# Attention over 32 batch items: LayerNorm pieces, value and key units and the text keys' scores in other places of a step

## The chip, the cores and the metric

The kernel runs on one core of a Trainium2 chip. Its five engines are named as in the profile: PE (TensorE, matmuls; PEld are its weight loads), DVE (VectorE), ACT (ScalarE), POOL (GpSimd) and SP (SyncE, which here only issues DMAs). Each works through a list of its own in order and waits on semaphores. The metric is the device time of one execution in microseconds (us); lower is better.

## What is computed

A state-space kernel gives 128 image rows per batch item, 77 text rows are put behind them, and these 205 rows go through causal attention and a linear layer with a Fourier adapter:

```python
h = _L0_tok_ref(L0_tok_log_dt, L0_tok_Lambda, x, 1024)      # (32, 128, 1024)
h = jnp.concatenate([h, txt], axis=1)                       # (32, 205, 1024)
h = h + _L0_attn_ref(_layernorm(h, axis=-1), wq, wk, wv, wo)
h = h + _L0_ffn_ref(_layernorm(h, axis=-1), W_base, b_base, ...)
```

The attention has 32 query heads of 32 channels and 8 key/value heads, so 4 query heads share a key head. The softmax is over the keys j <= i.

## The kernel before

The program has three stages: `ssm` (the state-space part), `attention`, and `tail` (output projection and linear layer). The change is in the first two, nearly all of it in `attention`.

**Steps and slots.** `attention` is software-pipelined over the batch. Step b (from -4 to 32) works on several items at once: attention proper of item b ("att"), row maxima of item b+1 ("max"), projections of item b+2 ("qkv"), transposes of item b+3 ("turn"), LayerNorm of item b+4 ("ln"), the load of item b+5. A step has eight slots g, one for each key head. Every float32 operand is split into a high and a low float16 part, and a product is three matmuls.

**PE in slot g.** The list of a slot: `scores(g, 0)` and `scores(g, 1)` (transposed scores, image keys, L981; called S0 and S1 here), `score_rows(g, 0)` and `(g, 1)` (scores for the row maxima, L1024 and L1028: M0, M1), the first half of a projection unit (FRONT, 12 matmuls), `scores(g, 2)` (text keys, L984: S2), `score_rows(g, 2)` (M2, which begins with L1028), the second half (BACK), `weigh(g-1)` (weights times values, 36 small matmuls: W), and then the slot's further units. A unit is 24 matmuls of 205 columns. Each slot has a query unit; `EXTRA` adds a value or key unit to four slots, and two "m" units (two small transposes each) stand in slots 0 and 4.

**The two banks of the transposed scores.** S0, S1 and S2 write PSUM banks `psT` in turn, so each waits until ACT's exponential has read the bank two before it:

```python
wait(pe, exp_done, 24 * b + 3 * g + k - 1)
ps = psT[(g + k) % 2]
```

So S2 of slot g waits for the exponential of part 0 of g, and S1 of slot g+1 waits for the exponential of part 2 of g.

**ACT in slot g** takes the exponentials of the three parts (L783), copies the three parts to their high float16 half (L790) once POOL has masked them, then copies the slot's units out of PSUM (L798). `high_part` (L732, L734: centre and scale half a row tile) stands behind slots 4 to 7. ACT's queue also issues `load`, `store` and `values` (the two copies L742).

**POOL in slot g** masks the three parts (`affine_select`, L699), each when its exponential is there, and then takes the low half of parts 1 and 2 (L704). After slot 3 it runs `scale_rows`: twelve small operations for 1/sqrt(variance) and one for the mean (L1135 to L1138, L673).

**DVE in slot g** reduces M0 (L879), M1, takes the low half of the unit left over from the slot before (L893), reduces M2, takes the low half of part 0 (L936), does its LayerNorm work (`layer_norm` in slots 1 to 3; `low_part`, L862, in slots 6, 7 and 0), normalizes W's result of slot g-1, and splits the slot's units but the last. In slot 7 it splits the last one too, before the M0 of the next step:

```python
if m < len(rows[g]) - 1 or g == NKV - 1:
    split_unit(*late)
```

**SP** restacks keys and queries, issues the DMA transposes of the LayerNorm output (`turn`) and of the values, and shifts the maxima rows. At step 30 it issues fifteen loads for the tail (`ahead`).

## Time and profile before

| what | value |
|---|---|
| three runs, us | 2894.34, 2895.55, 2897.94 (median 2895.55) |
| the profiled execution, its time, us | 2894.3 |
| its span, us | 2891.9 |
| PE busy, share of the span | 92% |
| DVE, ACT, POOL busy, share of the span | 67%, 43%, 40% |
| mean granted PE clock | 0.975 of full |

Some 2.4 us lie around the span. Busy shares are means over three stages that differ: in the attention loop all four engines have much to do, in the tail PE works nearly alone.

### The profile page before, as it was taken

What the parts mean: (1) busy time and instruction counts of PE and PEld (TensorE: products, weight loads), DVE (VectorE), ACT (ScalarE), POOL (GpSimd) and SP (SyncE); (2) the same over time, 40 slices, a digit from 0 to 9 for tenths busy, and PEclk for the clock granted to TensorE, in tenths of its full rate; (3) what the DMA queues carried; (4) which work ended last, traced back from release to release, by engine and by line L of the source; (5) the groups of instructions that cost most, each with busy time, mean ns of one, the idle gap of its engine ahead of it and who ended that gap; (6) DMA issues with size and microseconds to landing.
All of it is one profiled execution on the core that took longest, in us unless ns stands there. A gap on an engine that the chain in (4) does not pass through costs nothing. (4 is left out here: it accounts for less than half of the span.)

```text
span 2891.9 us, 70053 instructions
## 1 busy us (share of the span) xinstructions
PE 2655.3 (92%) x27456; PEld 1919.6 (66%) x27456; DVE 1941.2 (67%) x5569; ACT 1230.0 (43%) x2570; POOL 1144.9 (40%) x1810
## 2 busy tenths in 40 slices
PE   1948999999999999999999976999999999999999
PEld 1838888888888888888888952444444444444444
DVE  8966888888888888888888674644444444444443
ACT  4343676766767676766667572201000010101010
POOL 2751565656656565666656570101010101010100
PEclk9979999999999999999999976999999999999999
DMA  7756556465555555565555454454545455545553
GB/s 242 194 122 100 98 92 105 85 109 93 96 94 96 103 93 104 84 107 92 101 92 86 73 124 170 113 139 116 133 122 136 119 134 121 133 123 131 125 129 77
DMA packets 509031, 332.99 MB, mean 115 GB/s; under 512 B 421145, under 2 KB 464409, under 8 KB 508225
## 3 DMA queue, kind: packets, MB, share of 16 engines
q1 hardware_dynamic: 486192, 264.68, 46.3%
q10 hardware_dynamic: 22512, 63.84, 7.1%
q8 instruction: 219, 3.59, 0.6%
q14 instruction: 108, 0.88, 0.1%
HBM read 116.49 MB, written 80.61 MB: 68 GB/s over the span
## 5 line engine op out<-in xcount | busy, mean ns | idle before, releaser
L1044 PE MATMUL psJ<-xth,qh 128*128 128x205 f16 x2048 | 517.3, 253 | 51.6 <-DMA xtl<-xfl 47.6
L704 POOL TENSOR_TENSOR pl<-arena,ph 128x410 f16<-128x410 f32 (+1 forms) x512 | 501.0, 998 | 94.7 <-ACT ph L790 94.7
L1046 PE MATMUL psJ<-xth,ql 128*128 128x205 f16 x2048 | 516.3, 252 | 0.0
L1045 PE MATMUL psJ<-xtl,qh 128*128 128x205 f16 x2048 | 515.8, 252 | 0.0
L699 POOL TENSOR_SCALAR_AFFINE_SELECT arena<-arena 128x256 f32<-128x256 f32 (+1 forms) x768 | 331.7, 438 | 438.3 <-ACT arena L783 419.3
L1261 POOL TENSOR_TENSOR arena<-stage,arena 128x1024 f32<-128x1024 f32 x52 | 122.1, 2349 | 936.2 <-DVE stage L1304 936.2
L1275 ACT CAST xh<-arena 128x1024 f16<-128x1024 f32 x52 | 54.3, 1045 | 995.1 <-DVE arena L1313 995.1
L783 ACT ACTIVATE arena<-psT,escale 128x410 f32<-128x410 f32 (+1 forms) x768 | 399.6, 565 | 95.5 <-PE psT L984 57.5
L790 ACT CAST ph<-arena 128x410 f16<-128x410 f32 (+1 forms) x768 | 334.8, 500 | 14.9 <-POOL arena L699 14.7
L1304 DVE SCALAR_TENSOR_TENSOR stage<-ps5O,osc,h_in 128x512 f32<-128x512 f32 x104 | 77.9, 750 | 388.4 <-PE ps5O L1401 388.4
L885 DVE TENSOR_REDUCE mx<-psS 77x2 f32<-77x410 f32 x512 | 296.5, 579 | 60.7 <-PE psS L1031 57.0
L1399 PE MATMUL ps5F<-wfh,xth 128*128 128x512 f16 x832 | 315.4, 379 | 3.4 <-DMA xtl<-xl 2.3
L1400 PE MATMUL ps5O<-wol,ath 128*128 128x512 f16 x832 | 316.1, 380 | 0.0
L1399 PE MATMUL ps5O<-woh,ath 128*128 128x512 f16 x832 | 316.1, 380 | 0.0
L1401 PE MATMUL ps5O<-woh,atl 128*128 128x512 f16 x832 | 316.0, 380 | 0.0
L1400 PE MATMUL ps5F<-wfl,xth 128*128 128x512 f16 x832 | 315.3, 379 | 0.0
L1401 PE MATMUL ps5F<-wfh,xtl 128*128 128x512 f16 x832 | 315.3, 379 | 0.0
L879 DVE CUSTOM_DVE_ANT_0 seen<-psS,mask 128x128 bf16<-128x128 f32 x1024 | 235.4, 286 | 82.7 <-PE psS L1024 82.0
L1010 PE MATMUL psO<-vh,ph 128*128 128x33 f16 (+1 forms) x3072 | 261.0, 178 | 5.0 <-issue 4.6
L1010 PE MATMUL psO<-vl,ph 128*128 128x33 f16 (+1 forms) x3072 | 260.0, 178 | 0.0
L1010 PE MATMUL psO<-vh,pl 128*128 128x33 f16 (+1 forms) x3072 | 260.0, 178 | 0.0
L1046 PE MATMUL psJ<-xth,kl 128*128 128x205 f16 x1024 | 257.8, 252 | 0.0
(231 smaller groups left out, 6106.2 us busy)
## 6 DMA issues: line engine op xcount, KB each, us to landing
a_in<-acat SPq DMA_DIRECT2D x52, 512.0 KB, 3.8
h_in<-hcat SPq DMA_DIRECT2D x52, 512.0 KB, 4.6
qst<-qsh SPq DMA_DIRECT2D x128, 205.0 KB, 4.7
out<-stage SPq DMA_DIRECT2D x51, 512.0 KB, 3.1
hcat<-ob SPq DMA_DIRECT2D x64, 256.0 KB, 4.4
xin<-hcat ACTq DMA_DIRECT2D x32, 512.0 KB
acat<-arena ACTq DMA_DIRECT2D x64, 256.0 KB
qst<-qsl SPq DMA_DIRECT2D x64, 205.0 KB, 5.7
```

What stands on the lines that cost most here:

```text
L699: pool.affine_select(out=v, in_=v, compare_op=ALU.is_ge, fill=0.0, base=0, pattern=[[0, v.shape[1]], [1, w]], channel_multiplier=-1).then_ ...
L704: pool.tensor_tensor(view(pl, g % 2, k), view(p32, g % 2, k), view(ph, g % 2, k), ALU.subtract).then_inc(lo_pool, 1)
L783: act.activation(view(p32, g % 2, k), ps_view(psT[(g + k) % 2], k), ACT.Exp, scale=(escale[:, 0:1] if k < 2 else escale[0:TXT, 0:1])).then ...
L790: act.copy(view(ph, g % 2, k), view(p32, g % 2, k)).then_inc(hi_done, 1)
L885: dve.tensor_reduce(dst, v, AX.X, ALU.max).then_inc(s_read, 1)
L1010: m = pe.matmul(o[:, t, r, :], p, v[0:T[j], j, g, :], start=n == 0, stop=n == len(list_) - 1)
L1044: pe.matmul(ps[:, 0:S], wh[:, k, c], xth[:, par, k, 0:S], start=k == 0, stop=False)
L1045: pe.matmul(ps[:, 0:S], wh[:, k, c], xtl[:, par, k, 0:S], start=False, stop=False)
L1046: m = pe.matmul(ps[:, 0:S], wl[:, k, c], xth[:, par, k, 0:S], start=False, stop=k == KC - 1)
L1399: pe.matmul(ps[h][:], th[:, k, :], wh[:, k, c], start=k == 0, stop=False)
L1400: pe.matmul(ps[h][:], th[:, k, :], wl[:, k, c], start=False, stop=False)
L1401: m = pe.matmul(ps[h][:], tl[:, k, :], wh[:, k, c], start=False, stop=k == KC - 1)
```

## The change

Four edits in `attention`, and one at its border with `ssm`.

1. `EXTRA` moves the value and key units from slots 0 to 3 to slots 1 to 4. `HIGH`, `LOW` and `LINK` set the LayerNorm pieces: ACT's `high_part` behind slots 1, 2 and 3 (two pieces there), DVE's `low_part` in slots 2, 3 and 4 (two pieces there), the statistics in slots 1 to 3. They now work on item b+3 in the step in which it is transposed, so `rs` and `nmean` have two buffers. POOL's `scale_rows` moves from behind slot 3 to behind slot 4.
2. On PE, S2 moves behind M2 and BACK.
3. On ACT the exponential of part 2 moves behind the high copies of parts 0 and 1. On POOL the low half of part 1 moves ahead of the mask of part 2.
4. `load` and `store` are issued by SP and not by ACT, `values` is split over slots 1 and 2, and SP's list is reordered; the loads for the tail are spread over the steps from 1 on.
5. Before the loop the first item's LayerNorm is done by DVE alone, its pieces come ahead of half of the weights' low parts, and item 0 is loaded alone. In `ssm` the weight peaks are taken two chunks earlier, and their way through memory starts a chunk earlier.

```diff
             for dst, src, arrived in ahead:
                 sp.dma_start(dst, src).then_inc(arrived, 16)
             for ch in range(NCH):
-                if ch == NCH - 1:
-
+
+                if ch == NCH - 2:
                     sp.wait_ge(peaks_ok, 1)
                     sp.dma_start(acat[0, 0:2 * P].rearrange("(p t) -> p t", t=2), peaks[:]).then_inc(peaks_out, 16)
+                if ch == NCH - 1:
                     sp.wait_ge(peaks_out, 16)
                     sp.dma_start(all_peaks, acat[0:1, 0:2 * P].broadcast_to([P, 2 * P])).then_inc(peaks_in, 16)
 
...
-        EXTRA = {0: ("v", 0), 1: ("v", 1), 2: ("k", 0), 3: ("k", 1)}
+        EXTRA = {1: ("v", 0), 2: ("v", 1), 3: ("k", 0), 4: ("k", 1)}
+
+
+        HIGH, LOW, LINK = {1: (0,), 2: (1,), 3: (2, 3)}, {2: (0,), 3: (1,), 4: (2, 3)}, {1: 0, 2: 1, 3: 2}
...
+                if has["last"]:
+                    store(b - 1, 1)
                 if has["qkv"]:
 
...
+                if has["turn"]:
+
+                    wait(sp, pj_filled, base)
+                    turn(0, nxt, b + 3)
+                if has["qkv"]:
+
+                    wait(sp, pj_lo, base + at(rows, "k", 0) + 1)
+                    wait(sp, st_filled, 24 * b + 12)
+                    restack(K_PARTS, kst[par][:, 0:4], slice(0, 1), k_in[0])
+                    wait(sp, pj_lo, base + at(rows, "q", 3) + 1)
+                    restack(Q_PARTS, qst[par][:, 0], HALVES[0], q_in[0])
+                if has["turn"]:
+                    turn(1, nxt, b + 3)
                 if has["max"]:
 
                     wait(sp, pj_lo, base + at(rows, "m", 0) + 1)
                     shift_rows(0, nxt)
+                if has["att"]:
+                    store(b, 0)
+                if has["load"]:
+                    sp.wait_ge(x_lo, 4 * (b + 4))
+                    load(b + 5, 1 - par)
+                if 1 <= b < len(ahead):
+                    dst, src, arrived = ahead[b]
+                    sp.dma_start(dst, src).then_inc(arrived, 16)
+                if b == B - 3:
+
+                    for q in v_in:
+                        sp.wait_ge(q, 32 * B)
+                    dst, src, arrived = ahead[0]
+                    sp.dma_start(dst, src).then_inc(arrived, 16)
+
...
+            load(0, 0)
+            sp.wait_ge(x_in[0], 32)
+            load(1, 1)
...
+            def causal(b, g, k):
+                pool.wait_ge(exp_done, 24 * b + 3 * g + k + 1)
+                v = view(p32, g % 2, k)
+                v = v[:, :, 0:P] if k < 2 else v
+                w = v.shape[2]
+                pool.affine_select(out=v, in_=v, compare_op=ALU.is_ge, fill=0.0, base=0,
+                                   pattern=[[0, v.shape[1]], [1, w]], channel_multiplier=-1).then_inc(masked, 1)
+
+            def low_weights(b, g, k):
+                pool.wait_ge(hi_done, 24 * b + 3 * g + k + 1)
+                pool.tensor_tensor(view(pl, g % 2, k), view(p32, g % 2, k), view(ph, g % 2, k),
+                                   ALU.subtract).then_inc(lo_pool, 1)
 
...
-                    for k in range(3):
-                        pool.wait_ge(exp_done, 24 * b + 3 * g + k + 1)
-                        v = view(p32, g % 2, k)
-                        v = v[:, :, 0:P] if k < 2 else v
-                        w = v.shape[2]
-                        pool.affine_select(out=v, in_=v, compare_op=ALU.is_ge, fill=0.0, base=0,
-                                           pattern=[[0, v.shape[1]], [1, w]],
-                                           channel_multiplier=-1).then_inc(masked, 1)
-                    for k in (1, 2):
-                        pool.wait_ge(hi_done, 24 * b + 3 * g + k + 1)
-                        pool.tensor_tensor(view(pl, g % 2, k), view(p32, g % 2, k), view(ph, g % 2, k),
-                                           ALU.subtract).then_inc(lo_pool, 1)
-                    if g == 3 and has["ln"]:
+                    causal(b, g, 0)
+                    causal(b, g, 1)
+                    low_weights(b, g, 1)
+                    causal(b, g, 2)
+                    low_weights(b, g, 2)
+                    if g == 4 and has["ln"]:
                         scale_rows(b)
 
...
+            def exponential(b, g, k):
+                act.wait_ge(st_filled, 24 * b + 3 * g + k + 1)
+
+                if k:
+                    wait(act, lo_pool, 16 * b + 2 * (g - 2) + k)
+                else:
+                    wait(act, lo_done, 8 * b + g - 1)
+                act.activation(view(p32, g % 2, k), ps_view(psT[(g + k) % 2], k), ACT.Exp,
+                               scale=(escale[:, 0:1] if k < 2 else escale[0:TXT, 0:1])).then_inc(exp_done, 1)
+
+            def high_weights(b, g, k):
+                act.wait_ge(masked, 24 * b + 3 * g + k + 1)
+                act.copy(view(ph, g % 2, k), view(p32, g % 2, k)).then_inc(hi_done, 1)
+
...
                 if b == -3:
+                    for n in range(4):
+                        high_part(0, n)
...
-                    if g == 3 and has["load"]:
-                        act.wait_ge(x_lo, 4 * (b + 4))
-                        load(b + 5, 1 - par)
-                    if g == 2 and has["last"]:
-                        store(b - 1, 1)
-                    if g == 2 and has["max"]:
-                        values(b + 1)
-                    if g == 6 and has["att"]:
-                        store(b, 0)
                     if has["att"]:
-                        for k in range(3):
-                            act.wait_ge(st_filled, 24 * b + 3 * g + k + 1)
-
-                            if k:
-                                wait(act, lo_pool, 16 * b + 2 * (g - 2) + k)
-                            else:
-                                wait(act, lo_done, 8 * b + g - 1)
-                            act.activation(view(p32, g % 2, k), ps_view(psT[(g + k) % 2], k), ACT.Exp,
-                                           scale=(escale[:, 0:1] if k < 2 else escale[0:TXT, 0:1])
-                                           ).then_inc(exp_done, 1)
-
+                        exponential(b, g, 0)
+                        exponential(b, g, 1)
                         wait(act, av_done, 8 * b + g - 1)
-                        for k in range(3):
-                            act.wait_ge(masked, 24 * b + 3 * g + k + 1)
-                            act.copy(view(ph, g % 2, k), view(p32, g % 2, k)).then_inc(hi_done, 1)
+                        high_weights(b, g, 0)
+                        high_weights(b, g, 1)
+                        exponential(b, g, 2)
+                        high_weights(b, g, 2)
+                    if g in (1, 2) and has["max"]:
+                        values(b + 1, g - 1)
...
-                    if g >= 4 and has["ln"]:
-                        high_part(b, par, g - 4)
+                    if has["turn"] and b > -3:
+                        for piece in HIGH.get(g, ()):
+                            high_part(b + 3, piece)
...
-                    if has["turn"] and g == 0:
-                        low_part(b + 3, 3)
-                    if has["ln"]:
-                        if g in (1, 2, 3):
-                            layer_norm(b, par, g - 1)
-                        if b == -4 and g == 3:
-                            weights_low(0)
-                        for piece in {6: (0,), 7: (1, 2)}.get(g, ()):
-                            low_part(b + 4, piece)
-                        if b == -3 and g == 0:
-                            weights_low(1)
+                    if b == -3 and g == 0:
+                        for part, ks in (((0, 1), (4, 5)), ((2, 3), (6, 7))):
+                            for piece in part:
+                                low_part(0, piece)
+                            weights_low(0, ks)
+                        weights_low(1, range(KC))
+                    if has["turn"] and b > -3:
+                        for piece in LOW.get(g, ()):
+                            low_part(b + 3, piece)
+                    if has["ln"] and g in LINK:
+                        layer_norm(b, par, LINK[g])
+                    if b == -4 and g == NKV - 1:
+                        weights_low(0, range(4))
...
                     project(0, FRONT)
+                    maxes(groups[:1], (2,))
+                    project(0, BACK)
                     if has["att"]:
                         scores(b, par, g, 2)
-                    maxes(groups[:1], (2,))
-                    project(0, BACK)
                     maxes(groups[1:], (0, 1))
                     if has["att"] and g:
                         weigh(b, par, g - 1)
```

Where the rows stand now. The names are those of the program: `arena` holds the exponentials in float32, `ph` and `pl` their high and low float16 parts, `psJ` a unit, `qsh`, `ksh` and `mh` its high part. ACT, from the end of slot 3 into slot 5, before:

```order
L798 CAST ksh<-psJ 128x205
L783 ACTIVATE arena<-psT,escale 128x410 x2
L783 ACTIVATE arena<-psT,escale 77x308
L790 CAST ph<-arena 128x410 x2
L790 CAST ph<-arena 77x308
L798 CAST qsh<-psJ 128x205
L796 ACTIVATE mh<-psJ 16x205
L732 ACTIVATE xin<-xin,nmean 128x512
L734 ACTIVATE xfh<-xin,rs 128x512
L783 ACTIVATE arena<-psT,escale 128x410 x2
```

The same place after, from the end of slot 3 through slot 4:

```order
L826 CAST ksh<-psJ 128x205
L761 ACTIVATE xin<-xin,nmean 77x512
L763 ACTIVATE xfh<-xin,rs 77x512
L761 ACTIVATE xin<-xin,nmean 77x512
L763 ACTIVATE xfh<-xin,rs 77x512
L785 ACTIVATE arena<-psT,escale 128x410 x2
L790 CAST ph<-arena 128x410 x2
L785 ACTIVATE arena<-psT,escale 77x308
L790 CAST ph<-arena 77x308
L826 CAST qsh<-psJ 128x205
L826 CAST ksh<-psJ 128x205
L824 ACTIVATE mh<-psJ 16x205
```

Two pieces of row work now stand ahead of slot 4's exponentials, and the third exponential stands between the second and the third high copy.

POOL around `scale_rows` (`rs` holds its intermediate values), before, the end of slot 3 and the start of slot 4:

```order
L704 TENSOR_TENSOR pl<-arena,ph 128x410
L704 TENSOR_TENSOR pl<-arena,ph 77x308
L1135 TENSOR_TENSOR rs<-rs 128x2
...
L673 TENSOR_SCALAR nmean<-mv 128x2
L699 AFFINE_SELECT arena<-arena 128x2x128 x2
L699 AFFINE_SELECT arena<-arena 77x308
L704 TENSOR_TENSOR pl<-arena,ph 128x410
```

After, the end of slot 4 and the start of slot 5:

```order
L720 TENSOR_TENSOR pl<-arena,ph 77x308
L1172 TENSOR_TENSOR rs<-rs 128x2
...
L706 TENSOR_SCALAR nmean<-mv 128x2
L715 AFFINE_SELECT arena<-arena 128x2x128 x2
L720 TENSOR_TENSOR pl<-arena,ph 128x410
L715 AFFINE_SELECT arena<-arena 77x308
L720 TENSOR_TENSOR pl<-arena,ph 77x308
```

The thirteen small operations stand one slot later, and the low half of part 1 is ahead of the text keys' mask.

## Rows read from the trace of the kernel before

**Rows 1.** The page's first line.
```profile
span 2891.9 us, 70053 instructions
```

**Rows 2.** Windows: steps 0 to 27, and step 31. Columns: busy time (x instructions), clock.
```profile
286.80:1588.90 1302.10, 1227.55 (x19119) 1148.37 (x19117) 1072.87 (x3666) 896.80 (x2019) 799.06 (x1483) 1.00 0.56 96
...
1712.10:1740.00 27.90, 18.95 (x314) 10.97 (x314) 21.79 (x37) 22.85 (x49) 23.73 (x39) 0.50 0.09 32
```

**Rows 3.** Timeline, PE, steps 13 and 14. Columns: start, length, line, what.
```profile
898.26 0.51 PE L981 MATMUL psT<-qst,kst 98*128 98x410 f16 x2
...
904.62 0.51 PE L981 MATMUL psT<-qst,kst 98*128 98x410 f16 x2
...
918.61 0.51 PE L981 MATMUL psT<-qst,kst 98*128 98x410 f16 x2
...
923.03 0.51 PE L981 MATMUL psT<-qst,kst 98*128 98x410 f16 x2
...
925.46 0.33 PE L984 MATMUL psT<-qst,kst 98*77 98x308 f16 x1 [0.19 <-ACT arena L783]
...
927.84 0.51 PE L981 MATMUL psT<-qst,kst 98*128 98x410 f16 x2
...
937.07 0.51 PE L981 MATMUL psT<-qst,kst 98*128 98x410 f16 x2
...
938.96 0.30 PE L984 MATMUL psT<-qst,kst 98*77 98x308 f16 x1
...
940.34 0.23 PE L1028 MATMUL psS<-mask,ident_bf 77*77 77x154 bf16 x1 [1.09 <-DVE mx L879]
```

**Rows 4.** Timeline, ACT, the end of slot 3 to slot 6, step 13.
```profile
918.81 0.33 ACT L798 CAST ksh<-psJ 128x205 f16<-128x205 f32 x1 [2.39 <-PE psJ L1046]
...
921.76 1.32 ACT L790 CAST ph<-arena 128x410 f16<-128x410 f32 x3 [0.41 <-POOL arena L699]
...
923.46 0.70 ACT L732 ACTIVATE xin<-xin,nmean 128x512 f32<-128x512 f32 x1
...
924.83 1.51 ACT L783 ACTIVATE arena<-psT,escale 128x410 f32<-128x410 f32 x3
926.24 1.30 ACT L790 CAST ph<-arena 128x410 f16<-128x410 f32 x3
927.45 0.32 ACT L798 CAST qsh<-psJ 128x205 f16<-128x205 f32 x1
```

**Rows 5.** Timeline, POOL, slots 3 to 7 of step 13.
```profile
917.77 0.19 POOL L1135 TENSOR_TENSOR rs<-rs 128x2 f32<-128x2 f32 x1
...
921.09 0.22 POOL L673 TENSOR_SCALAR nmean<-mv 128x2 f32<-128x2 f32 x1
921.26 1.22 POOL L699 TENSOR_SCALAR_AFFINE_SELECT arena<-arena 128x256 f32<-128x256 f32 x3
...
925.48 1.42 POOL L699 TENSOR_SCALAR_AFFINE_SELECT arena<-arena 128x256 f32<-128x256 f32 x3 [0.98 <-ACT arena L783]
927.28 1.70 POOL L704 TENSOR_TENSOR pl<-arena,ph 128x410 f16<-128x410 f32 x2 [0.38 <-ACT ph L790]
...
936.01 3.12 POOL L704 TENSOR_TENSOR pl<-arena,ph 128x410 f16<-128x410 f32 x2 [0.38 <-ACT ph L790]
```

**Rows 6.** Timeline, DVE: before the loop, then slot 7 into slot 0.
```profile
209.00 0.75 DVE L862 SCALAR_TENSOR_TENSOR xfl<-xin,rs,xfh 128x512 f16<-128x512 f32 x1 [3.09 <-ACT xfh L734]
...
938.99 0.36 DVE L893 TENSOR_TENSOR qsl<-psJ,qsh 128x205 f16<-128x205 f32 x1
939.27 0.28 DVE L879 CUSTOM_DVE_ANT_0 seen<-psS,mask 128x128 bf16<-128x128 f32 x1
```

**Rows 7.** Timeline, POOL, ACT and PE, before the first unit.
```profile
196.31 1.29 POOL L1135 TENSOR_TENSOR rs<-rs 128x2 f32<-128x2 f32 x1 [1.18 <-DVE rs L1128]
...
207.50 0.72 ACT L732 ACTIVATE xin<-xin,nmean 128x512 f32<-128x512 f32 x1 [10.90 <-POOL nmean L673]
...
223.92 0.33 PE L1044 MATMUL psJ<-xth,qh 128*128 128x205 f16 x1 [47.64 <-DMA xtl<-xfl]
```

More of the change, by code:

```diff
@@ L814, in _, with weights_low @@
             dve.wait_ge(cleared, 1)
-            def weights_low(n):
-                for k in range(KC):
+            def weights_low(n, ks):
+                for k in ks:
                     dve.wait_ge(w_hi, n * KC + k + 1)
```

95 lines of the change are left out of this document (47 added, 48 removed).

## The prediction

> **What bounds the kernel now.** I read the page first, for the span and the busy shares [rows 1], then the windows by step [rows 2], then the timeline of PE over one step, slot by slot [rows 3], and for each place where PE stops, the timelines of the engines that it stops for [rows 4 to 6]. The reader is to see that the attention loop is PE's, but not fully. Steps 0 to 27 take 1302.1 us, 46.50 each, at clock 1.00 [rows 2]. A slot with a query unit and a value unit, in which PE never stops, takes 6.36 (904.62 less 898.26), slot 4, with a query and an m unit, 4.42 (923.03 less 918.61) [rows 3]. With some 0.18 for the m unit (my estimate; it is two tiny transposes), a bare query slot is 4.24 and an extra unit 2.12. A step's work is then 8 x 4.24 + 4 x 2.12 + 2 x 0.18 = 42.76. PE stands still for the other 3.74. Two of the places are in the rows: S2 of slot 5 waits for an exponential that comes late because ACT did row work first, and M2 of slot 0, at 940.34, waits 1.09 for DVE, whose list was long with `low_part` [rows 3]. All the change can win in the loop is 3.74 x 28 = 105 us, since the work is the same after it.
>
> **The chain that the change makes.** Let X be the start of a slot's first exponential. Before, the three exponentials stand together (1.51 for three, so one each 0.51), and the high copies behind them wait for little. After, the order is exponentials 0 and 1, high copies 0 and 1, exponential 2, high copy 2, and POOL has the low half of part 1 ahead of mask 2. Step by step: the second exponential starts at X + 0.51; its mask 0.65 later (925.48 less 924.83) at X + 1.16; the copy behind a mask starts 0.50 after it (921.76 less 921.26), so high copy 1 at X + 1.66 [rows 4, 5]. Exponential 2 follows at the copies' pitch of 0.43, X + 2.09. POOL's low half of part 1 starts 0.61 after its copy (927.28 less 926.24 and 0.43), at X + 2.27, and takes about 0.97 of the pair's 1.70 (410 columns of 718) [rows 5]. Mask 2 at X + 3.24, high copy 2 at about X + 3.8, low half 2 from X + 4.3 to X + 5.05, the query unit's copy at X + 4.15, and the next slot's first exponential at **X + 4.37**. PE needs 4.24 for a bare slot. So in slots 5 to 7 this chain is no faster than PE and cannot make up for a delay. Before, ACT's own list for such a slot was 1.51 + 1.30 and one small copy, some 3.0 [rows 4], and it could. What waits for it: an S matmul follows its exponential's start by 0.63 (925.46 less 924.83) [rows 3, 4]; S1 of the next slot needs exponential 2, so it stands at X + 2.72 or later.
>
> **Slot 4 to slot 6.** ACT copies the key unit at 0.20 after the slot's start (918.81 less 918.61), and 0.23 later comes to the two pieces that `HIGH` puts behind slot 3, 1.37 each (924.83 less 923.46) [rows 3, 4]. So X = 3.16 into slot 4. S2, which stood 1.89 into a slot (938.96 less 937.07), stands M2 and BACK later, at 3.2, and waits until 3.8: a stall of 0.6. Then POOL: low half 2 ends at X + 5.05, and now `scale_rows` begins and holds POOL from 917.77 to 921.26, 3.49 [rows 5]. Mask 0 of slot 5 cannot start before X + 8.6. Before, that pause cost PE nothing, since all exponentials stood ahead of the masks. Now exponential 2 of slot 5 stands behind high copy 1, and S1 of slot 6 waits for it: mask 0 to exponential 2 is 2.09 - 0.65 = 1.44, and 0.63 more, so X + 10.7, 13.85 after slot 4's start. PE would be there after 4.42 + 2.12 + 4.24 + 0.17 = 10.95. Stall: **2.9** in all, the 0.6 among it.
> To this comes contention. DVE's two `low_part` now run in slot 4 while POOL takes its low halves. In slot 7 of before the two met, and POOL's pair took 3.12 for 1.70 [rows 5]. Here POOL is on the chain. Bounds 0 and 1.42; I take 1.0, near the measured end, since the same instructions meet.
> The Trainium skill, page SBUF — State Buffer, Who interferes with whom, says that a DVE instruction with two SBUF inputs and a GpSimd instruction that reads SBUF exclude each other for a whole instruction, whoever comes first. By it the price is a whole number of `low_part`s, and two of them would give 1.5 and 2977 in all, none 2935. The pair's growth of 1.42, two pieces of 0.75 less a little, agrees with that.
>
> **Slot 7 to slot 0.** S1 of slot 6 being bound by the chain, X of slot 6 is 4.37 - 2.72 = 1.65 behind it, X of slot 7 another 4.37, slot 7's query copy 4.15 behind that. DVE splits this unit before the M0 of the next step: it starts 0.37 after the copy's start (estimate: the copy's 0.33 and a semaphore), and 0.28 later the M0 reduction starts (939.27 less 938.99), and M2 stands 1.07 behind that (940.34 less 939.27) [rows 3, 4, 6]. Sum 11.9. PE's own way is 2 x 4.24 + 1.89 - 0.17 = 10.2. Stall: **1.7**. The wait of before at the same M2 has another cause, the late `low_part`s, and that one goes.
>
> **Slots 1 to 3.** These are the long slots, and ACT's one piece fits. DVE gets a `low_part` besides the statistics in slots 2 and 3. Its cost to PE is unknown: nothing if DVE's slack holds it, 1.1 if the piece with contention comes whole. I take 0.7, one piece alone (0.75) [rows 6], and 0.1 for slot 1.
>
> **What costs nothing.** `load` and `store` on SP: SP only waits and issues there, and its transposes and restacks have slots 5 to 7 before the next step needs them; without that cover PE would wait at the step's first unit. What ACT gains by not issuing them is in X already, and `values` in slots 1 and 2 is covered by the long slots (without it, 0.5 a slot).
>
> **The loop.** 2.9 + 1.0 + 1.7 + 0.7 + 0.1 = 6.4 of waiting, 42.76 + 6.4 = 49.2 a step for 46.50: 2.66 x 28 = **+74**. Steps 28 and 29 have no `scale_rows`; I leave them unchanged.
>
> **Start.** Before, POOL's rounds of item 0 ran slowly beside DVE's weights, the first at 1.29 for 0.19 in the loop [rows 5, 7], and ACT waited 10.90 for them; the first unit began at 223.92, behind 47.64 of idleness [rows 7]. After, DVE does them itself; at POOL's pitch in the loop that would be 3.5 in all for 10.9, loads item 0 alone and its pieces first. 7 to 9 from the rounds and some 3 from the load and the earlier pieces: **-12**. Bounds: 0, if the first unit waits for the weights' low halves, and -15.
>
> **End.** Step 31 takes 27.9 with eight slots, 3.5 each [rows 2]. PE has little there, and the chain without the query copy is 4.15: 0.65 x 8 = **+5**. Bounds 0 and 8.
>
> **Sum.** 2894.3 (the profiled execution: a span of 2891.9 [rows 1] and 2.4 around it) + 74 - 12 + 5 = 2961.3. The median of the runs shown is 1.25 above the profiled execution: **2963**.
>
> **Rivals.**
> Rival A, faster: the pause of `scale_rows` does not reach PE. Then X of slot 5 is early (under 1), S1 of slot 6 does not wait, X drifts up by 0.13 a slot, and M2 of slot 0 waits about 1.0. Waiting is 0.6 + 1.0 + 0.7 + 0.1 = 2.4, a step 45.2, and the sum 2894.3 - 37.5 - 12 + 5, with the 1.25, is 2851. For it: POOL idles 0.98 before its masks in slot 6 and the pause was free before [rows 5]. Against it: the order of the two lists leaves exponential 2 no way round mask 1. It decides at 3.74 + 0.25 = 4.0 of waiting a step; below that the kernel is faster.
> Rival B, slightly slower: the stalls are as above but lie over one another, DVE's lie within ACT's, and contention is nil: 2.9 + 1.7 = 4.6, 0.86 x 28 = 24, and 2913.
> Rival C, no change: new stalls of about 4.0 take the place of the old 3.74, and start and end nearly cancel. 2895.
> Rival D, worse: both unknowns at their upper ends, 1.42 and 1.1: 7.2 of waiting, 3.5 x 28 = 97, and 2986. Against it: a stall of DVE's and one of ACT's in neighbouring slots partly cover each other.
>
> **How the numbers follow.** The forecast (2925 to 2990) has 0.50, B 0.15, D 0.07, C 0.07, A and what lies between it and no change 0.21. A measurement of this kernel can tell about 0.2%, 5.8 us, from no change. Slower 0.72, within it 0.07, faster 0.21. Range 2882 to 2993: it leaves out most of A and half of D. The forecast's own range is 2925 to 2990.
>
> **What would show it in the profile after.** Right: steps of about 49; PE's largest waits are psT for ACT's exponential, at S1 of slot 6 and S2 of slot 4; POOL's masks of slot 5 directly behind L706; M2 of slot 0 waits 1.5 or more for DVE, DVE for the copy of slot 7's unit. The first unit starts near 212. Wrong: S1 never waits for L785; DVE's `low_part` in slot 4 at 0.75 beside POOL's low half at 0.97; steps under 46.5. The steps most at risk are the 4.37 of the chain (0.2 less in each slot and the 1.7 falls to 1.1) and the 0.7 for DVE.

## The result: 2.5% slower, and the profile after

The changed kernel takes 2969.26 us (median of 4 runs, 2965.74 to 2975.67), the kernel before, run beside it, 2896.48 (2894.34 to 2897.94): 1.0246 times as long, 95% interval 1.0228 to 1.0264. The forecast was 2963. The profiled execution is the longest of the four, 6.4 above the median, and the one of the kernel before is the shortest of its four, 2.1 below; so differences of the two profiles are 8.5 too large in sum.

Page and windows of the kernel after (columns as in [rows 2]); the stretches are the first units to step 0 in two parts, steps 0 to 27, and step 31:

```profile
span 2973.9 us, 70146 instructions
...
PE 2671.1 (90%) x27456; PEld 1928.3 (65%) x27456; DVE 1921.4 (65%) x5582; ACT 1252.0 (42%) x2570; POOL 1142.9 (38%) x1797
```
```profile
211.50:236.00 24.50, 18.82 (x167) 17.10 (x168) 15.45 (x34) 4.77 (x10) 4.11 (x19) 0.84 0.12 38
236.00:288.00 52.00, 46.03 (x494) 44.17 (x491) 29.34 (x114) 15.00 (x33) 4.97 (x23) 0.93 0.66 107
288.00:1655.88 1367.88, 1229.96 (x19116) 1150.45 (x19117) 1050.90 (x3663) 915.45 (x2015) 805.48 (x1482) 1.00 0.49 93
...
1782.00:1812.30 30.30, 17.75 (x283) 9.98 (x279) 17.09 (x35) 19.56 (x43) 21.29 (x35) 0.50 0.08 29
```

The loop is where the time went: 1367.9 for 1302.1 [rows 2], 48.85 a step for 46.50, at the same clock 1.00 and with nearly the same work of PE (1230.0 busy for 1227.6). So 65.8 of the span's 82.0 are lost in the loop, nearly all of it by standing still. Groups of PE by line in that stretch (columns: busy, mean ns, then idle time ahead of them and its releasers), first after, then before:

```profile
L1081 PE MATMUL psJ<-xth,qh 128*128 128x205 f16 x1792 | 453.0, 253 | 34.1 <-DVE qsl L928 34.1
L1018 PE MATMUL psT<-qst,kst 98*128 98x410 f16 x448 | 120.4, 339 | 17.1 <-ACT arena L785 14.6 <-DMA qst<-ml 2.5
L1065 PE MATMUL psS<-mask,ident_bf 77*77 77x154 bf16 x448 | 104.6, 233 | 31.4 <-DVE mx L914 31.4
L1021 PE MATMUL psT<-qst,kst 98*77 98x308 f16 x224 | 67.6, 302 | 12.6 <-ACT arena L785 12.6
L1089 PE MATMUL psJ<-ident,mx 128*16 128x128 f32 x56 | 15.3, 274 | 42.8 <-DVE qsl L928 42.8
```
```profile
L1028 PE MATMUL psS<-mask,ident_bf 77*77 77x154 bf16 x448 | 104.2, 233 | 38.7 <-DVE mx L879 38.7
L984 PE MATMUL psT<-qst,kst 98*77 98x308 f16 x224 | 69.3, 309 | 35.1 <-ACT arena L783 33.1 <-DVE mx L885 0.2
```

138.0 of waiting for 73.8: the 64.2 between them is nearly the whole of the loop's loss. Two of the five lines are waits that before did not have, 34.1 and 42.8, both for L928, DVE's split of a unit (`split_unit`): a query unit of slots 1 and 3, and the m unit of slot 4, each of which needs the `psJ` bank that the query unit before holds until it is split. Together they are 76.9, more than half of all waiting.

Where a step waits is seen from the starts of S0. Length of each slot in us (median over steps 3 to 26), beside the work of 4.24 a slot, 2.12 an extra unit and 0.18 an m unit, and the mean step over steps 0 to 27. The "tables" are `EXTRA`, `HIGH`, `LOW` and `LINK` (edit 1), the "orders" are edits 2 and 3, and the two rows of work are what the slots would take without waits:

| kernel | g0 | g1 | g2 | g3 | g4 | g5 | g6 | g7 | step |
|---|---|---|---|---|---|---|---|---|---|
| work, units as after | 4.42 | 6.36 | 6.36 | 6.36 | 6.54 | 4.24 | 4.24 | 4.24 | 42.76 |
| after | 5.87 | 6.94 | 6.36 | 7.32 | 8.87 | 4.24 | 4.91 | 4.25 | 48.85 |
| e1 old orders, new tables | 4.56 | 6.56 | 6.95 | 6.98 | 9.41 | 4.24 | 4.24 | 4.24 | 47.22 |
| e3 no rounds on POOL | 5.22 | 6.94 | 6.36 | 7.32 | 8.87 | 4.24 | 4.25 | 4.24 | 47.49 |
| e4 POOL's order back | 5.04 | 6.86 | 6.36 | 6.57 | 9.07 | 4.25 | 4.74 | 4.24 | 47.64 |
| e5 pieces spread | 5.37 | 6.94 | 6.36 | 7.32 | 7.24 | 4.24 | 6.14 | 4.24 | 47.89 |
| e11 best | 4.55 | 6.93 | 6.95 | 6.94 | 7.12 | 4.24 | 4.23 | 4.24 | 45.23 |
| e12 best, S2 late in g1 to g4 | 4.55 | 6.36 | 8.16 | 8.14 | 8.31 | 4.24 | 4.75 | 4.24 | 48.80 |
| work, units as before | 6.54 | 6.36 | 6.36 | 6.36 | 4.42 | 4.24 | 4.24 | 4.24 | 42.76 |
| before | 7.82 | 6.36 | 7.30 | 6.36 | 4.41 | 4.82 | 4.50 | 4.73 | 46.50 |
| e2 new orders, old tables | 9.78 | 6.36 | 6.36 | 6.36 | 4.42 | 6.32 | 5.18 | 6.05 | 51.40 |

Timeline of PE after, step 14, which answers to [rows 3]: the starts of slots 0, 4 and 5, and the six places where PE stands still (in slots 0, 1, 3, 4 twice, and S1 of slot 6 in the last line).

```profile
972.26 0.52 PE L1018 MATMUL psT<-qst,kst 98*128 98x410 f16 x2
...
975.68 0.23 PE L1065 MATMUL psS<-mask,ident_bf 77*77 77x154 bf16 x1 [1.37 <-DVE mx L914]
...
979.66 0.26 PE L1081 MATMUL psJ<-xth,qh 128*128 128x205 f16 x1 [0.41 <-DVE qsl L928]
...
993.33 0.26 PE L1081 MATMUL psJ<-xth,qh 128*128 128x205 f16 x1 [0.78 <-DVE qsl L928]
...
998.87 0.51 PE L1018 MATMUL psT<-qst,kst 98*128 98x410 f16 x2
...
1002.68 0.33 PE L1021 MATMUL psT<-qst,kst 98*77 98x308 f16 x1 [0.45 <-ACT arena L785]
...
1007.56 0.28 PE L1089 MATMUL psJ<-ident,mx 128*16 128x128 f32 x1 [1.53 <-DVE qsl L928]
...
1007.74 0.51 PE L1018 MATMUL psT<-qst,kst 98*128 98x410 f16 x2
...
1012.82 0.35 PE L1018 MATMUL psT<-qst,kst 98*128 98x410 f16 x1 [0.50 <-ACT arena L785]
```

The chain from slot 4 to slot 6 on ACT (beside [rows 4]), POOL ([rows 5]) and DVE ([rows 6]), each a timeline:

```profile
1002.05 1.07 ACT L785 ACTIVATE arena<-psT,escale 128x410 f32<-128x410 f32 x2
1003.20 0.97 ACT L790 CAST ph<-arena 128x410 f16<-128x410 f32 x2
1004.08 0.51 ACT L785 ACTIVATE arena<-psT,escale 77x308 f32<-77x308 f32 x1
1006.15 0.45 ACT L790 CAST ph<-arena 77x308 f16<-77x308 f32 x1 [1.57 <-POOL arena L715]
1006.50 0.32 ACT L826 CAST qsh<-psJ 128x205 f16<-128x205 f32 x1
...
1008.18 1.06 ACT L785 ACTIVATE arena<-psT,escale 128x410 f32<-128x410 f32 x2
1011.38 0.97 ACT L790 CAST ph<-arena 128x410 f16<-128x410 f32 x2 [2.14 <-POOL arena L715]
1012.26 0.51 ACT L785 ACTIVATE arena<-psT,escale 77x308 f32<-77x308 f32 x1
...
1014.45 1.09 ACT L785 ACTIVATE arena<-psT,escale 128x410 f32<-128x410 f32 x2
...
1018.70 1.09 ACT L785 ACTIVATE arena<-psT,escale 128x410 f32<-128x410 f32 x2
```
```profile
1004.25 0.97 POOL L720 TENSOR_TENSOR pl<-arena,ph 128x410 f16<-128x410 f32 x1 [0.66 <-ACT ph L790]
1005.17 0.95 POOL L715 TENSOR_SCALAR_AFFINE_SELECT arena<-arena 77x308 f32<-77x308 f32 x1
1006.68 0.77 POOL L720 TENSOR_TENSOR pl<-arena,ph 77x308 f16<-77x308 f32 x1 [0.56 <-ACT ph L790]
1007.40 0.19 POOL L1172 TENSOR_TENSOR rs<-rs 128x2 f32<-128x2 f32 x1
...
1010.71 0.22 POOL L706 TENSOR_SCALAR nmean<-mv 128x2 f32<-128x2 f32 x1
1010.89 0.77 POOL L715 TENSOR_SCALAR_AFFINE_SELECT arena<-arena 128x256 f32<-128x256 f32 x2
```
```profile
1004.27 2.38 DVE L897 SCALAR_TENSOR_TENSOR xfl<-xin,rs,xfh 77x512 f16<-77x512 f32 x2
...
1007.14 0.36 DVE L928 TENSOR_TENSOR qsl<-psJ,qsh 128x205 f16<-128x205 f32 x1
...
1023.08 0.37 DVE L928 TENSOR_TENSOR qsl<-psJ,qsh 128x205 f16<-128x205 f32 x1 [1.08 <-ACT qsh L826]
```

The reader is to see one chain. X, the start of slot 4's first exponential, is 1002.05, 3.18 into the slot, behind two pieces; the rounds begin at 1007.40 and end with the mean at 1010.71; mask 0 of slot 5 follows at 1010.89; exponential 2 of slot 5 cannot start before 1012.26, and S1 of slot 6 stands 0.56 behind it, at 1012.82.

### The profile page after: what moved, and what is told of

Read it like the earlier page. It is cut to its first block and busy times, and to the rows that moved or that the text cites. A ratio compares the mean times of both kernels' runs of the same rounds, so it can differ in the third digit from the quotient of the medians.

```text
span 2973.9 us, 70146 instructions
## 1 busy us (share of the span) xinstructions
PE 2671.1 (90%) x27456; PEld 1928.3 (65%) x27456; DVE 1921.4 (65%) x5582; ACT 1252.0 (42%) x2570; POOL 1142.9 (38%) x1797
## 5 line engine op out<-in xcount | busy, mean ns | idle before, releaser
L720 POOL TENSOR_TENSOR pl<-arena,ph 128x410 f16<-128x410 f32 (+1 forms) x512 | 484.9, 947 | 318.0 <-ACT ph L790 318.0
L790 ACT CAST ph<-arena 128x410 f16<-128x410 f32 (+1 forms) x768 | 362.8, 504 | 371.6 <-POOL arena L715 353.5
L715 POOL TENSOR_SCALAR_AFFINE_SELECT arena<-arena 128x256 f32<-128x256 f32 (+1 forms) x768 | 373.2, 488 | 289.3 <-ACT arena L785 273.8
L785 ACT ACTIVATE arena<-psT,escale 128x410 f32<-128x410 f32 (+1 forms) x768 | 406.3, 562 | 69.4 <-PE psT L1021 65.9
L1081 PE MATMUL psJ<-xth,kh 128*128 128x205 f16 x1024 | 257.5, 252 | 2.0 <-DVE qsl L928 2.0
```

The source lines that it names most:

```text
L715: pool.affine_select(out=v, in_=v, compare_op=ALU.is_ge, fill=0.0, base=0, pattern=[[0, v.shape[1]], [1, w]], channel_multiplier=-1).then_ ...
L720: pool.tensor_tensor(view(pl, g % 2, k), view(p32, g % 2, k), view(ph, g % 2, k), ALU.subtract).then_inc(lo_pool, 1)
L785: act.activation(view(p32, g % 2, k), ps_view(psT[(g + k) % 2], k), ACT.Exp, scale=(escale[:, 0:1] if k < 2 else escale[0:TXT, 0:1])).then ...
L790: act.copy(view(ph, g % 2, k), view(p32, g % 2, k)).then_inc(hi_done, 1)
L1081: pe.matmul(ps[:, 0:S], wh[:, k, c], xth[:, par, k, 0:S], start=k == 0, stop=False)
```

## The experiments

Times are medians; the ratio is to the kernel before, run in the same sittings (2896.8 to 2899.9).

**e1, the three orders back.** Edits 2 and 3 undone (S2 on PE, exponential 2 on ACT, low half 1 on POOL); tables, SP's list and start stay as after. PE's part (ACT's and POOL's left out):

```diff
                     project(0, FRONT)
+                    if has["att"]:
+                        scores(b, par, g, 2)
                     maxes(groups[:1], (2,))
                     project(0, BACK)
-                    if has["att"]:
-                        scores(b, par, g, 2)
```


> The changed kernel with the three orders of before: S2 between the halves of the unit, three exponentials together, POOL's masks ahead of its low halves. The moved row work and SP's new list stay. Chain theory (the new orders cost the time): about 46.6 us a step for 48.85, some 2900 us; what is left is a wait of about 1.9 at S2 of slot 4, whose exponential stands behind two pieces of row work, and 0.5 at S2 of slots 2 and 3. Rival (the moved row work overloads DVE in slots 2 to 4, and the orders are free): no change, 2960 or more.


Measured: 2908.29, ratio 1.0029 (1.0018 to 1.0039), 47.22 a step. The orders cost 61 of the 73 us; in the loop, 1.63 of the 2.35 a step. PE's wait at S1 for an exponential is gone, S2's is larger.

**e2, the orders alone.** The kernel before with edits 2 and 3 and nothing else. ACT's part:

```diff
...
+                        exponential(b, g, 0)
+                        exponential(b, g, 1)
                         wait(act, av_done, 8 * b + g - 1)
...
+                        high_weights(b, g, 0)
+                        high_weights(b, g, 1)
+                        exponential(b, g, 2)
+                        high_weights(b, g, 2)
```


> The kernel before with only the three new orders, row work, units and queues as before. Chain theory: a chain of 4.4 and a piece of row work of 1.37 make 5.8 us a slot in slots 4 to 7, where PE needs 4.24, so some 4 us a step more: about 3015 us. Rival (DVE's list is the cause): within 15 us of before, 2896.


Measured: 3047.65, ratio 1.051 (1.0494 to 1.0525), 51.40 a step. With e1 this makes a square: tables alone +0.71 a step (with SP's new list, which e1 keeps), orders alone +4.90, both +2.35. The new tables thus take back two thirds of what the orders cost: with the old ones the pieces and the late split meet in slots 5 to 7, which have no extra unit to hide them (6.32, 5.18 and 6.05 for 4.24), and in slot 0, which has a `low_part` of its own (9.78 for 6.54).

**e3, no rounds.** `scale_rows` leaves out its twelve rounds from step 0 on, so the rows' scale is not worked out.

```diff
-                rsqrt_rounds(links, pool, rs[:, b % 2])
+                if b < 0:
+                    rsqrt_rounds(links, pool, rs[:, b % 2])
```


> The changed kernel without the twelve rounds for 1/sqrt(variance) on POOL from step 0 on (it leaves that part of the LayerNorm out; the mean stays). Chain theory: the pause behind slot 4 shrinks from 3.5 to 0.3 us, the 0.67 at S1 of slot 6 goes and some 1.0 of the wait at M2 of slot 0, since the chain then starts early: 1.7 a step, about 2920 us. Slot 4 itself (8.87) stays, because its m unit waits for DVE. Rival (DVE alone sets the stalls): less than 10 us faster than 2969.


Measured: 2934.8, ratio 1.0116 (1.0101 to 1.0131), 47.49 a step. Slot 6 falls from 4.91 to 4.25, slot 0 from 5.87 to 5.22. The pause is worth 1.37 a step and no more, since slot 4 stays at 8.87: its m unit waits whether the rounds are there or not, and that wait had eaten most of the chain's.

**e4, POOL's order back.** Mask 2 ahead of the low half of part 1, all else as after.

```diff
                     causal(b, g, 1)
+                    causal(b, g, 2)
                     low_weights(b, g, 1)
-                    causal(b, g, 2)
```


> The changed kernel with POOL's mask of the text keys ahead of its low half of the image keys again, ACT and PE as changed. Chain theory: high copy 2 and the unit's copy come 0.5 us earlier in each slot, so DVE can split it earlier: M2 of slot 0 waits 0.5 less and the query units of slots 1 and 3 some 0.3 each, about 1.1 a step, 2938 us. Rival (POOL's list from mask 0 to its last low half is as long in either order and sets the pace alone): no change, 2969.


Measured: 2938.41, ratio 1.0134 (1.0118 to 1.0151), 47.64 a step. The sum is as expected, 31 us for which of two small instructions POOL takes first; its parts are not. Expected were 0.5 in slot 0 and 0.3 each in slots 1 and 3; slot 0 gives 0.83, slot 1 0.08 and slot 3 0.75, and slot 4 loses 0.20. There is a second way that this order helps, beside the earlier copies: DVE's `low_part` now meets mask 2 and not POOL's low half. In slots 2 and 3 it takes 0.75 here, for 1.49 in after, and the query unit of slot 3 waits for the split that stands behind slot 2's piece. The run does not part the two. The loop ran at a mean granted clock of 0.98 here, PE busy 1244.0 for 1230.0 after, so without that the order would be worth some 14 more.

**e5, pieces spread.** One piece a slot, no slot with two (`LINK` stands in the same line and stays).

```diff
-        HIGH, LOW, LINK = {1: (0,), 2: (1,), 3: (2, 3)}, {2: (0,), 3: (1,), 4: (2, 3)}, {1: 0, 2: 1, 3: 2}
+        HIGH, LOW, LINK = {1: (0,), 2: (1,), 3: (2,), 4: (3,)}, {2: (0,), 3: (1,), 4: (2,), 5: (3,)}, {1: 0, 2: 1, 3: 2}
```


> The changed kernel with its two-piece places spread: `high_part` one piece each behind slots 1, 2, 3 and 4, `low_part` one each in slots 2, 3, 4 and 5. Theory: slot 4 is 8.87 long because two pieces stand ahead of its first exponential (at +3.17) and because its m unit waits 1.7 for the split of its query unit, which DVE takes behind two low parts. With one piece each, the first exponential comes some 1.4 earlier, S2's 0.6 goes, about 0.9 of the m unit's wait goes, and slot 6's S1 goes with them: 1.5 less a step, 47.3 a step, about 2927. Rival: the pieces move the pressure to slot 5; the piece behind slot 4 stands ahead of slot 5's exponential, so S1 of slot 6 stays 13.9 behind slot 4's start: steps of 48.8, 2968.


Measured: 2945.12, ratio 1.0157 (1.0142 to 1.0172), 47.89 a step. Between the theory and the rival. Slot 4 gains 1.63, slot 6 loses 1.23 (S1 and M2 both wait there): most of what slot 4 gains comes out again two slots later, as it must if slots 5 to 7 cannot make up for a delay.

**e6, the query unit's copy and split early.** ACT copies it ahead of exponential 2; DVE splits it ahead of its row work in slots with more than one unit. ACT's part:

```diff
                         high_weights(b, g, 1)
+                        if rows[g] and rows[g][0][0] == "q":
+                            copy_unit(b, par, base, k0, n, rows[g][0])
+                            n += 1
                         exponential(b, g, 2)
```


> The changed kernel, but ACT copies the slot's query unit ahead of exponential 2, and DVE splits it, in slots with more than one unit, ahead of its row work. Theory: three waits have one cause, that the query unit's split comes late: M2 of slot 0 (1.32), the second units of slots 1 and 3 (1.52) and the m unit of slot 4 (1.7). All of them shrink; I count 0.8 of the total 4.5 for slots 1 and 3 each covered, so 3.0 less a step: 45.9, about 2886. Rival: exponential 2 now stands behind a copy that waits for BACK, and S1 of each next slot waits for exponential 2: 0.35 more in each of the slots 5 to 7 and 0, so the gain is half eaten, 47.3, 2925, or all eaten, 48.9, 2968.


Measured: 2937.78, ratio 1.0134 (1.0119 to 1.0149), 47.73 a step. Groups of PE in steps 0 to 27:

```profile
L1093 PE MATMUL psJ<-xth,qh 128*128 128x205 f16 x1792 | 461.3, 257 | 14.6 <-DVE ksl L935 14.6
L1030 PE MATMUL psT<-qst,kst 98*128 98x410 f16 x450 | 121.5, 340 | 51.8 <-ACT arena L785 49.5 <-DMA qst<-ml 2.3
L1077 PE MATMUL psS<-mask,ident_bf 77*77 77x154 bf16 x448 | 106.9, 239 | 12.5 <-DVE mx L921 10.6
```

The waits for DVE fall from 108.3 (34.1, 31.4 and 42.8) to 25.2, as the theory said, and S1's wait for exponential 2 grows from 14.6 to 49.5, as the rival said: the gain is 1.12 a step for the theory's 3.0. Part of the rest is the clock, 0.98 in this loop as in e4 (matmuls of 257 ns for 253 after).

**e7, three edits.** e4 and e5 together, and one round behind each of slots 4, 5 and 6. The third edit, at its call:

```diff
-                    if g == 4 and has["ln"]:
-                        scale_rows(b)
+                    if g in (4, 5, 6) and has["ln"]:
+                        scale_rows(b, (g - 4,))
```


> The changed kernel with three edits: one piece a slot (as in the run with spread pieces), POOL's mask 2 ahead of its low half of part 1 (that alone gave 47.64 a step), and the rounds of `scale_rows` one each behind slots 4, 5 and 6 with the mean behind slot 6. Theory: the waits are separate, so the gains add: 47.64 less 1.4 for the rounds and 1.3 for slot 4, 45.0 a step, 2865, and faster than the kernel before. Rival: the gains are of one and the same stall, and the step stays near 46.5 to 47: 2905 to 2920.


Measured: 2927.73, ratio 1.0099 (1.0084 to 1.0115), 47.39 a step. The theory fell, and the step is longer than the rival's too. S1 waits for exponential 2 again (46.6 in the loop), now in slots 7 and 0 and not in slot 6. Whether the gains were of the same stall, or the rounds behind slots 5 and 6 made a new one there, this run does not tell.

**e8, five edits.** e7 with e6's copy and split. ACT's part of the two:

```diff
                         high_weights(b, g, 1)
+                        if rows[g] and rows[g][0][0] == "q":
+                            copy_unit(b, par, base, k0, n, rows[g][0])
+                            n += 1
                         exponential(b, g, 2)
```


> The kernel with three edits and the early copy and split of the query unit as well. Theory: 1.5 to 2 a step less than with three edits, about 43.3, next to the 42.76 of work, 2818 to 2830. Rival: with the three edits DVE and ACT have slack at those places already, so the early copy gives nothing, or costs 0.3 a slot behind exponential 2: 45 to 46 a step, 2865 to 2890.


Measured: 2898.55, ratio 1.0004 (0.9994 to 1.0013), 46.50 a step: no better than before. S1's wait is 58.5. Both the theory and the rival were too hopeful.

**e9, the old orders and the pieces spread.** e1 and e5 together. After e7 and e8 the suspicion was that the orders, not the places, kept the step up.

```diff
-        HIGH, LOW, LINK = {1: (0,), 2: (1,), 3: (2, 3)}, {2: (0,), 3: (1,), 4: (2, 3)}, {1: 0, 2: 1, 3: 2}
+        HIGH, LOW, LINK = {1: (0,), 2: (1,), 3: (2,), 4: (3,)}, {2: (0,), 3: (1,), 4: (2,), 5: (3,)}, {1: 0, 2: 1, 3: 2}
```


> The changed kernel with all three old orders (as in the run with the orders back, 2908, 47.22 a step) and the pieces spread, `high_part` behind slots 1, 2, 3, 4 and `low_part` in slots 2, 3, 4, 5. Theory: in the run with the orders back all but 1.2 of the waiting stands in slot 4 (9.41 for 6.54 of work): S2 waits 1.81 since two pieces stand ahead of its exponential, and the m unit waits for a split behind two low parts. One piece each takes 2.2 of it; a piece ahead of slot 5's exponential costs 0.5. 45.5 a step, 2860, faster than the kernel before. Rival: as in the three-edit run, the wait goes elsewhere and the step stays at 46.5 to 47: 2890 to 2905.


Measured: 2881.16, ratio 0.9945 (0.9925 to 0.9965), 46.11 a step. Faster than before, by less than half of what the theory gave; slots 5 and 6 lose 0.6 and 0.5 to the moved piece, which ACT now has ahead of slot 5 and DVE in it.

**e10, pieces one slot earlier.** As e9, with every piece a slot earlier; the line against after's:

```diff
-        HIGH, LOW, LINK = {1: (0,), 2: (1,), 3: (2, 3)}, {2: (0,), 3: (1,), 4: (2, 3)}, {1: 0, 2: 1, 3: 2}
+        HIGH, LOW, LINK = {0: (0,), 1: (1,), 2: (2,), 3: (3,)}, {1: (0,), 2: (1,), 3: (2,), 4: (3,)}, {1: 0, 2: 1, 3: 2}
```


> The same with the pieces one slot earlier: `high_part` behind slots 0, 1, 2, 3, `low_part` in slots 1, 2, 3, 4, so that every piece on ACT falls ahead of the exponential of a long slot (1 to 4). Theory: the 0.5 in slot 5 goes too: 45.0 a step, 2846. Rival: DVE now has a low part beside the statistics in each of the slots 1 to 3, and the second units there wait for their splits by 0.5 each: 46.2, 2880.


Measured: 2860.7, ratio 0.9871 (0.9854 to 0.9888), 45.29 a step. Slots 5 to 7 are at 4.24, the bare work. The first S0 stands at 290.8, for 287.7 in e9, so the time gained 20 on e9 where the steps gained 23.

**e11, split ahead of the normalization.** e10, and DVE splits the query unit first in slots with more than one unit.

```diff
+                    first = len(rows[g]) > 1
+                    if first:
+                        split_unit(b, par, (k0 + n) % 2, *rows[g][0], base + n + 1)
+                        n += 1
                     if has["att"] and g:
                         norm(b, par, g - 1)
```


> The same again, and in slots with more than one unit DVE splits the query unit ahead of the normalization of the slot before. Theory: what is left of the m unit's wait in slot 4 (0.6 to 0.7) is the normalization of 0.6 ahead of the split; it goes, and 0.5 to 0.7 less a step: 44.4, 2830. Rival: W of the next slot waits for the normalization (it needs the bank psO), and gets the 0.6: no change from the run before it.


Measured: 2854.65, ratio 0.9852 (0.9838 to 0.9867), 45.23 a step. This is the best version, 1.5% below the kernel before. The edit itself did next to nothing (0.06 a step): the 25.5 of waiting for splits are gone, and S2's wait for exponential 0 is 40.2 for 13.7. PE only came earlier to a place where it waits anyway.

**e12, S2 late in the long slots.** e11 with S2 behind M2 and BACK in slots 1 to 4.

```diff
-                    if has["att"]:
+                    if has["att"] and not 1 <= g <= 4:
                         scores(b, par, g, 2)
                     maxes(groups[:1], (2,))
                     project(0, BACK)
+                    if has["att"] and 1 <= g <= 4:
+                        scores(b, par, g, 2)
```


> The kernel of the run before it (pieces one slot early, split ahead of the normalization) and one thing of the change back: in slots 1 to 4 alone, S2 stands behind M2 and BACK. In those slots S2 waits 0.50 to 0.56 each, 2.1 a step, for exponential 0, which starts 1.8 into the slot behind a piece. Theory: this part of the change is good where it stands by itself and in the long slots; S2 then comes at 3.3, no longer waits, and 2.1 a step go: 43.1, 2796. Rival: exponential 2 now waits for S2, and the three high copies stand behind it, 0.6 later; the split of the query unit, the piece and the second units' bank come 0.6 later too, so PE waits 0.5 at the second units instead: 45.2, 2855.


Measured: 2957.7, ratio 1.0207 (1.019 to 1.0224), 48.80 a step: 103 us slower than e11. The rival's mechanism, at more than its price. The timeline of slot 1 (start 929.52 in e11, 976.98 in e12) shows it; DVE in e11:

```profile
933.29 0.58 DVE L971 TENSOR_TENSOR pl<-arena,ph 128x410 f16<-128x410 f32 x1
933.79 1.50 DVE L897 SCALAR_TENSOR_TENSOR xfl<-xin,rs,xfh 128x512 f16<-128x512 f32 x1
...
936.90 0.37 DVE L928 TENSOR_TENSOR qsl<-psJ,qsh 128x205 f16<-128x205 f32 x1
```

ACT and DVE in e12:

```profile
980.51 0.52 ACT L785 ACTIVATE arena<-psT,escale 77x308 f32<-77x308 f32 x1 [0.65 <-PE psT L1025]
980.93 1.31 ACT L790 CAST ph<-arena 128x410 f16<-128x410 f32 x3
```
```profile
981.48 0.59 DVE L971 TENSOR_TENSOR pl<-arena,ph 128x410 f16<-128x410 f32 x1 [1.54 <-ACT ph L790]
981.99 1.49 DVE L897 SCALAR_TENSOR_TENSOR xfl<-xin,rs,xfh 128x512 f16<-128x512 f32 x1
...
985.09 0.37 DVE L928 TENSOR_TENSOR qsl<-psJ,qsh 128x205 f16<-128x205 f32 x1
```

DVE in e12 idles 1.54 for the high copies that stand behind exponential 2, takes its low half 4.50 into the slot for 3.77, and splits the query unit 8.11 after the slot's start for 7.38. That is 1.75 into slot 2, where PE's next query unit needs the bank at 0.8. PE, there and in the whole loop:

```profile
985.52 0.26 PE L1085 MATMUL psJ<-xth,qh 128*128 128x205 f16 x1 [1.19 <-DVE qsl L928]
```
```profile
L1085 PE MATMUL psJ<-xth,qh 128*128 128x205 f16 x1792 | 453.0, 253 | 86.1 <-DVE qsl L928 86.1
```

Slot 2 being later for it, S2 of slot 2 is later still.

## Why the forecast was right, step by step

**The chain from slot 4 to slot 6: right to 0.1.** S2 of slot 4 stands at 3.81 (forecast 3.8), S1 of slot 6 13.95 after slot 4's start (1012.82 less 998.87; forecast 13.85), mask 0 of slot 5 at X + 8.84 (8.6), exponential 2 1.37 behind it (1.44). The stall of the two places is slot 4's 2.33 and slot 6's 0.67, 3.0 for the forecast 2.9. What the step did not name is a second wait on the way, the m unit's, for the split of slot 4's query unit. It costs nothing on top, because it lies inside the chain's 13.95; e3 shows it from the other side: with the pause gone slot 6 and slot 0 gain 0.66 and 0.65, slot 4 nothing, and the m unit's wait remains. So one of the forecast's signs failed: PE's largest wait is not psT for ACT's exponential (27.2 in the loop, 14.6 and 12.6) but the m unit's for the split (42.8).

**Contention: the term that was mis-sized.** I put 1.0 on POOL's part of the chain; the chain is 0.1 longer than forecast. The two did meet, but mostly the other engine paid. POOL's low half 1 keeps its 0.97 while the two `low_part` take 2.38 for 1.50; POOL lost only on mask 2, 0.95 for 0.50, which shows as 0.3 at high copy 2 (X + 4.10 for 3.8) and was nearly made up by steps that I had a little too long. The rule that the forecast cited from the Trainium skill (page SBUF — State Buffer, Who interferes with whom), that the two engines shut each other out for a whole instruction, agrees with these rows; what was wrong was to charge POOL for it. The rows of before that the forecast went by hold a different meeting. Timelines of DVE up to 937.0 and of POOL up to 937.5, before:

```profile
935.89 0.57 DVE L936 TENSOR_TENSOR pl<-arena,ph 128x410 f16<-128x410 f32 x1
936.39 0.74 DVE L862 SCALAR_TENSOR_TENSOR xfl<-xin,rs,xfh 128x512 f16<-128x512 f32 x1
```
```profile
936.01 1.94 POOL L704 TENSOR_TENSOR pl<-arena,ph 128x410 f16<-128x410 f32 x1 [0.38 <-ACT ph L790]
```

There POOL's low half 1 begins 0.12 behind DVE's own low half, and takes 0.97 longer than its own time: by these rows it waited out that instruction and the whole `low_part` behind it, which kept its 0.74. The forecast read the pair's 1.42 as two `low_part`s; it is this 0.97 and 0.45 at POOL's low half 2. In slot 4 of after, POOL's low half 1 begins when DVE's own (L971, 1003.76 to 1004.35) is nearly over, at 1004.25, and 0.02 ahead of the `low_part`.

**Slot 7 to slot 0: right in kind, 0.25 too much.** Slot 0 is 5.87 for 4.42, 1.45 for 1.7, and the row at 1023.08 shows DVE waiting 1.08 for the copy of slot 7's unit. The pitch of the exponentials in bare slots is 4.25 (1014.45, 1018.70), not 4.37, the step that the forecast had called most at risk.

**Slots 1 to 3: the place was wrong, and the size too small.** I had 0.8, as a wait of M2 for DVE. It is 0.58 in slot 1 and 0.96 in slot 3, and it is the query unit that waits for the split of the query unit before it in the same bank. This step was thought of by engines only, and not by banks. A part of it is contention again: the `low_part`s of slots 2 and 3 take 1.49 each, for the 0.75 that I counted.

**The loop.** 1.45 + 1.54 + 2.33 + 0.67 = 6.0 of waiting for 6.4, 65.8 in the loop for 74. The rivals: A (the pause does not reach PE) and B (stalls lie over one another, contention nil) are both out by S1 of slot 6, though B's second half was true; C is what e8 does, not this kernel; D had the slots 1 to 3 right, where 1.54 is even above its upper end, and contention wrong. One argument for A named the wrong slot: the masks at 925.48 [rows 5], before which POOL idles 0.98, are those of slot 5, which begins at 923.03 [rows 3]; nothing in the sum hangs on it.

**Start: wrong.** The first unit began at 211.56 for 223.92 [rows 7], 12.4 earlier, as forecast, but step 0 began at 288.0 for 286.8 [rows 2]. The two steps before it took 76.4 for 62.9: in these windows PE is busy 64.85 (before 59.52), 5.3 more for nearly the same units at granted clocks of 0.84 and 0.93 (before 0.93 and 1.00), and idle the other 8. In all eleven experiments with the new start the first unit stood at 210.4 to 213.9 and the first S0 at 285.1 to 291.4; with the old start (e2 and before) at 225.5 and 223.9, and 288.1 and 286.8. So an earlier start of PE bought nothing. The step that failed is that I followed the first unit and not step 0, which waits for all the restacks and maxima of two items. Why these two steps lengthen was not tried by itself, but the trace shows what ends last. In all twelve kernels with the new start the first S0 waits 2.3 to 4.0 (2.5 in after) for the DMA of `ml`, the low half of the maxima, and in before and e2 it does not. SP's row up to that DMA, after:

```profile
268.46 6.09 SPq L614 DMA_TRANSPOSE vt<-stage  x4
274.65 1.25 SPq L664 DMA_TRANSPOSE xth<-xfh  x1
...
284.94 0.59 SPq L659 DMA_DIRECT2D qst<-ml  x1
```

DVE has written `ml` at 278.78 (before 280.22), but SP, which issues without a break from 268.46, comes to it at 284.94 (before at 281.86). So `ml` waits 6.2 for its turn, for 1.6 before: in before its DMA stood right behind the transposes of the values, in SP's new list (edit 4) the two `turn`s and two restacks stand between. The forecast had called SP's list free; in the loop it is, at this place it is not. That another order of SP's list would bring the start's 12 back is not shown.

**End: too small.** From step 28 to the last S0 it is 156.4 for 147.2, +9 for my +5. The orders alone make it 158.3 (e2), the tables alone 139.6 (e1): the orders cost 11 to 17 there, and the tables give back 8. From the last S0 to the end of the span it is 1161.6 for 1155.8, and the experiments lie anywhere between the two, so no effect of the change can be read from that.

The errors of start (+13), end (+4), the stretch behind the last S0 (+6, which the forecast held unchanged) and loop (-8) leave 15; of these 6.4 are the profiled execution's distance above its median, where the forecast had put the median 1.25 above the profiled one, and 0.6 is time around the span (1.8 for 2.4). What is left is 6.3, 2969.26 for 2963. That it is so little is luck: the number came out better than its terms.

**What stays open.** S2's move and exponential 2's move were not taken apart in the changed kernel; e12 shows the first alone on another base. Nor was `load` and `store` on SP tried alone, and I can only say that no row of the loop shows PE waiting for a DMA but the 2.5 at the first S0.

## What to carry to other kernels

Moving one instruction down a list is also moving everything that stands behind its consumer on the next engine: S2 0.8 us later on PE (980.18 for 931.96, from the slots' starts) stopped ACT's in-order list, with it three copies, with them DVE's low half and split, and cost 103 us (e12), in slots that seemed to have room. When a pipeline's slots differ in length, put side work one piece at a time ahead of the long ones; and check every wait by the bank that it is for, since two engines' timelines do not show whose buffer is held. An earlier first instruction is worth only what the first instruction of the steady loop shows.

## What the runs showed of the hardware

A DVE piece and a POOL instruction that start together are not shared fairly. `low_part` of 128x512 takes 0.75 alone [rows 6] and 1.49 to 1.50 when it starts 0.01 to 0.02 behind POOL's low half (933.79 in e11, 981.99 in e12), while POOL's stays at 0.96 to 0.97. It was the same in all 665 such meetings in six kernels (after, e5, e9 to e12), 77 or 128 rows high, 1.49 to 1.50 each. So a row piece that begins with POOL's low half costs DVE double, and where DVE came first, as with mask 2 at 1005.17, POOL took 0.95 for 0.50. When POOL's low half begins in the middle of DVE's own low half it can lose to two DVE instructions in a row: 1.94 for 0.97 at 936.01 in before, and 1.93 to 1.95 in all 28 such places of that kernel, while the `low_part` behind kept its 0.74.

The granted clock can add to the price of waits. PE got 1.00 through the loop of after and of e11, but 0.98 in those of e4 and e6, whose longest waits in a step are little longer (some 1.7, in e4 at the m unit and in e6 at S1 of slot 6, for 1.53 after); there it took 14 and 17 us more for the same matmuls. In e2, with 1.96 at M2 of slot 0, it got 0.99. What set these apart the runs don't say. In the two steps ahead of the loop, after waits of 2 to 3.2, it got 0.84 and 0.93, and in step 31, where it is busy 59% of the time, 0.50, which is 1.2 GHz.
